# Weighing the expert activations on GpSimd and forming the low halves of the products on VectorE

## The chip, the cores and the metric

The kernel runs on one core of one Trainium2 chip. The metric is the device time of one execution in microseconds (us). The engines are TensorE (PE in the profile; PEld is its weight load), VectorE (DVE), ScalarE (ACT), GpSimd (POOL) and SyncE (SP, whose queue issues the DMAs). Each engine works through its own instructions in order, and semaphores order the engines among each other.

## What is computed

A gated linear attention layer and a mixture-of-experts feed-forward layer, each with a residual and a layer norm behind it. The input is 16 batches of 512 tokens of width 128. The change touches only the feed-forward part, in the reference:

```python
scores = jax.nn.softmax(xt @ gate_w.T, axis=-1)
topv, topi = jax.lax.top_k(scores, K)                 # K = 4 of E = 8 experts
topv = topv / jnp.sum(topv, axis=-1, keepdims=True)
combine = zeros((t, E)).at[arange(t)[:, None], topi].set(topv)
g = _silu(jnp.einsum('td,edh->eth', xt, exp_w1))
u = jnp.einsum('td,edh->eth', xt, exp_w3)
yexp = jnp.einsum('eth,ehd->etd', g * u, exp_w2)
routed = jnp.einsum('te,etd->td', combine, yexp)
shared = _silu(xt @ sh_w1) * (xt @ sh_w3) @ sh_w2     # two more experts' worth, not weighed
```

In front of it stand a linear and a gated layer (folded into one, "head"), behind it the same again ("tail"), then the second layer norm.

## The kernel before

The attention part runs first, for all 16 batches, and takes some 1,330 us. The expert stage follows, with one batch after the other. For each batch `n` it goes through ten slots `e` = 0 to 9: slots 0 and 1 are the two shared experts, slots 2 to 9 the eight routed ones. All tiles are 128 partitions by 512 tokens. In slot `e`:

- TensorE forms the two up projections, `up_gate` into `g_ps` and `up_linear` into `u_ps`, then the down projection `down` of the slot three back (`LAG` = 3). Each is three matmuls (L548 to L550), since every float32 operand is split into a high half and a low half: high by high, low by high, high by low.
- ScalarE takes silu of `g_ps` into `sg` (`silu_expert`, L1088), and then copies the product of the slot before, `gc`, into its high half `gc_part[0]` (`high_gc`, L1095).
- VectorE runs `gate_expert`: for a routed expert it multiplies `sg` by the combine weights `cw` (L1457, two inputs in SBUF), and then the result, or `sg` itself for a shared expert, by `u_ps` from PSUM (L1464), which gives `gc`.
- GpSimd subtracts the high half from `gc`, which gives the low half `gc_part[1]` (`low_gc`, L514, two inputs in SBUF).

Buffers tie the slots together: `sg`, `gu`, `g_ps` and `u_ps` are double, `gc` and its halves are fourfold. `up_linear` of slot `e` and silu of slot `e` wait for the product of slot `e` - 2; `down` of slot `e` - 3 waits for both halves. In the names of the trace `sq_sb` is `sg`, `kt_sb` and `s_sb` are `gu`, `v_sb` is `gc`, `wq` and `wk` (`_hi`, `_lo`) are `gc_part`, `ew_raw` and `e_sb` hold `cw`: the stage uses buffers of the attention part again.

Between the slots every engine does work for the neighbours. On VectorE, in this order, for the next batch: in slot 0 the low half of the head's input (L1374), in slot 2 the head's gated product (L1381, after `low_r`, L1393, of the batch before), in slot 3 its low half (L1388), in slot 4 the logits (L1401, L1404), in slots 5 to 7 the top-4 choice (L1417 to L1443, which ends with `comb`). For the batch before: in slot 3 the layer norm's output for two batches back (L1359, four instructions), in slot 6 the tail's gated product (L1593), in slots 8 and 9 the layer norm's sums and variance. ScalarE takes the exponential of the logits in slot 5 (L1082) and the tail's silu right behind it (L1110), each with a table load in front, and in slot 9 copies the transposed weights (L1100). SyncE stores these to DRAM and reads them back spread over all partitions into `cw` for slots 2 and up of the next batch (`spread_weights`, L389). GpSimd has one more instruction per batch, the `rstd` of the layer norm (L495), in slot 9.

## Time and profile before

| | us |
|---|---|
| median of 3 runs | 1809.33 (1806.43 to 1810.18) |
| the profiled execution | 1802.53 |
| its span, first to last instruction | 1800.8 |
| granted TensorE clock, mean | 0.994 of full speed |
| PE busy | 1673.4 (93%) |
| DVE busy | 1446.7 (80%) |
| ACT busy | 1107.5 (61%) |
| POOL busy | 614.3 (34%) |

The profile covers one execution. Busy shares are means over two very different stages, so they say little about the expert stage by themselves: there POOL is busy for about half of the time and DVE for more than eight tenths. The views that matter are those that can be asked for a stretch: the busy time per window, the waits, the chain that ended last in order of time, and the timeline of each engine. The durations of PE instructions are modelled and overlap; the start-to-start distance is the better measure of TensorE's pace.

### The profile page before, as it was taken

What the parts mean: (1) busy time and instruction counts of PE and PEld (TensorE: products, weight loads), DVE (VectorE), ACT (ScalarE), POOL (GpSimd) and SP (SyncE); (2) the same over time, 40 slices, a digit from 0 to 9 for tenths busy, and PEclk for the clock granted to TensorE, in tenths of its full rate; (3) what the DMA queues carried; (4) which work ended last, traced back from release to release, by engine and by line L of the source; (5) the groups of instructions that cost most, each with busy time, mean ns of one, the idle gap of its engine ahead of it and who ended that gap; (6) DMA issues with size and microseconds to landing.
All of it is one profiled execution on the core that took longest, in us unless ns stands there. A gap on an engine that the chain in (4) does not pass through costs nothing.

```text
span 1800.8 us, 83833 instructions
## 1 busy us (share of the span) xinstructions
PE 1673.4 (93%) x36615; PEld 1352.1 (75%) x36615; DVE 1446.7 (80%) x3326; ACT 1107.5 (61%) x2544; POOL 614.3 (34%) x470
## 2 busy tenths in 40 slices
PE   6999999999999999999999999999989999999996
PEld 5777777777777777777777778777777777777775
DVE  4888888787878878878878788877877888888886
ACT  5666566666666656666566666666655665666653
POOL 3323232232322233222322233222314554545544
PEclk9999999999999999999999999999999999999998
DMA  7000000000000000000000000000012322223222
GB/s 217 4 9 10 4 9 4 10 4 9 4 9 10 4 10 3 9 4 9 4 9 10 4 9 4 9 4 10 4 60 68 103 107 71 107 74 115 106 66 65
DMA packets 38139, 60.95 MB, mean 34 GB/s; under 512 B 3080, under 2 KB 24848, under 8 KB 37776
## 3 DMA queue, kind: packets, MB, share of 16 engines
q1 hardware_dynamic: 37776, 55.59, 9.3%
q8 instruction: 291, 4.77, 1.1%
q14 instruction: 72, 0.59, 0.1%
HBM read 46.93 MB, written 4.46 MB: 29 GB/s over the span
## 4 chain that ended last, share of the span: by engine, by line
PE 50%; DVE 24%; issue 11%; ACT 10%; DMA 3%; DVEq 0%; POOL 0%; ACTq 0%; SPq 0%; POOLq 0%
PE bank L641 7%; PE bank L548 7%; PE bank L676 6%; PE bank L550 6%; PE bank L549 6%; PE bank L690 5%; DVE k_sb L1283 5%; PE bank L587 4%; ACT v_sb L1017 3%; PE bank L663 3%; PE bank L624 3%; DVE kt_sb L1457 3%; DVE v_sb L1464 2%; DVE qq_sb L1283 2%; DMA ew_raw<-cw_dram 2%
## 5 line engine op out<-in xcount | busy, mean ns | idle before, releaser
L479 POOL TENSOR_TENSOR rn_sb<-ss_sb,expo 128x8 f32<-128x8 f32 x128 | 213.6, 1669 | 764.1 <-DVE ss_sb L1328 764.1
L1283 DVE TENSOR_TENSOR qq_sb<-qq_sb,tot_sb 128x512 f32<-128x512 f32 (+1 forms) x384 | 259.1, 675 | 231.7 <-PE bank L641 168.9
L1283 DVE TENSOR_TENSOR k_sb<-k_sb,tot_sb 128x512 f32<-128x512 f32 (+1 forms) x384 | 331.4, 863 | 1.3 <-PE bank L648 1.3
L1042 ACT ACTIVATE at_sb<-diag_sb 32x256 f32<-32x256 f32 x256 | 106.4, 416 | 164.8 <-DVE diag_sb L1295 160.1
L641 PEld LDWEIGHTS bank<-qq_sb,k_sb 128*32 128x32 f32 x12288 | 125.4, 110 | 62.9 <-issue 50.5
L514 POOL TENSOR_TENSOR wq_lo<-v_sb,wq_hi 128x512 fp32r<-128x512 f32 x80 | 112.2, 1406 | 132.7 <-ACT wq_hi L1095 132.7
L1017 ACT ACTIVATE v_sb<-bank,rn_sb 128x128 f32<-128x128 f32 x512 | 139.5, 384 | 26.6 <-PE bank L550 19.7
L323 POOL TENSOR_TENSOR tot_sb<-a_sb 128x512 f32<-128x512 f32 x64 | 96.1, 1502 | 167.0 <-ACT a_sb L1006 154.0
L641 PE MATMUL bank<-qq_sb,k_sb 128*32 128x16 f32 x12288 | 146.3, 185 | 6.9 <-issue 5.4
L548 PE MATMUL bank<-wg_hi,ew_hi 128*128 128x512 f32 x320 | 135.3, 423 | 15.8 <-DVE v_sb L1464 15.6
L690 PE MATMUL bank<-v_sb,at_sb 128*128 128x128 f32 x1024 | 148.1, 287 | 1.3 <-issue 1.0
L514 POOL TENSOR_TENSOR wk_lo<-v_sb,wk_hi 128x512 fp32r<-128x512 f32 x80 | 111.9, 1403 | 107.6 <-ACT wk_hi L1095 107.6
L587 PEld LDWEIGHTS bank<-ones_wide,sq_sb 128*32 128x32 f32 x8192 | 92.0, 111 | 62.0 <-issue 39.6
L1006 ACT ACTIVATE a_sb<-bank 128x512 f32<-128x512 f32 x128 | 76.6, 599 | 88.3 <-PE bank L550 79.6
L690 PEld LDWEIGHTS bank<-v_sb,at_sb 128*128 128x128 f32 x1024 | 124.2, 191 | 7.4 <-issue 1.7
L587 PE MATMUL bank<-ones_wide,sq_sb 128*32 128x1 f32 x8192 | 115.7, 173 | 11.6 <-issue 9.8
L549 PE MATMUL bank<-wg_lo,ew_hi 128*128 128x512 f32 x320 | 126.1, 394 | 0.0
L550 PE MATMUL bank<-wg_hi,ew_lo 128*128 128x512 f32 x320 | 126.1, 394 | 0.0
L1088 ACT ACTIVATE sq_sb<-bank 128x512 f32<-128x512 f32 x160 | 94.7, 592 | 49.5 <-PE bank L550 49.0
L676 PE MATMUL bank<-v_sb,kt_sb 128*128 128x128 f32 x768 | 119.9, 292 | 0.2
L700 PE MATMUL bank<-s_sb,qq_sb 128*128 128x128 f32 x768 | 113.3, 284 | 0.3
L988 ACT ACTIVATE k_sb<-bank 128x512 f32<-128x512 f32 x128 | 76.8, 600 | 55.3 <-PE bank L550 55.3
(195 smaller groups left out, 4254.3 us busy)
## 6 DMA issues: line engine op xcount, KB each, us to landing
ew_raw<-cw_dram SPq DMA_DIRECT2D x32, 768.0 KB, 6.2
x_nat<-in_L_attn_x_dram SPq DMA_DIRECT2D x16, 256.0 KB, 2.8
x_nat<-x_all SPq DMA_DIRECT2D x16, 256.0 KB, 2.5
ew_raw<-cw_dram SPq DMA_DIRECT2D x16, 256.0 KB, 3.9
e_sb<-cw_dram SPq DMA_DIRECT2D x16, 256.0 KB, 7.0
out_dram<-k_sb SPq DMA_DIRECT2D x16, 256.0 KB, 2.3
ew_raw<-in_L_ffn_exp_w_dram SPq DMA_DIRECT2D x3, 512.0 KB, 4.8
qq_sb<-in_L_attn_Wq_dram SPq DMA_DIRECT2D x1, 512.0 KB, 3.9
```

Source lines behind the costliest of these rows:

```text
L479: nc.gpsimd.tensor_tensor(rn_sb[par][:, i, :, :].rearrange("p h c -> p (h c)"), ss_sb[:, i * G:(i + 1) * G], expo[:, 0:G], ALU.pow).then_i ...
L514: nc.gpsimd.tensor_tensor(gc_part[1][(par * NE + e) % 4], gc[(par * NE + e) % 4], gc_part[0][(par * NE + e) % 4].bitcast(fp32), ALU.subtra ...
L548: nc.tensor.matmul(out_ap, stat(0), mov(0), start=start, stop=False)
L549: nc.tensor.matmul(out_ap, stat(0), mov(1), start=False, stop=False)
L550: return nc.tensor.matmul(out_ap, stat(1), mov(0), start=False, stop=stop)
L587: mm = nc.tensor.matmul((nb_ps, su_ps)[i][n * SB:(n + 1) * SB, col:col + 1], sq_sb[:, i * HP + h, lo:lo + SB], ones_wide[:, 0:1], start=Tr ...
L641: mm = nc.tensor.matmul(out[n * SB:(n + 1) * SB, g * HB:(g + 1) * HB], k_sb[par][:, left:left + SB], halves(qd_sb[par][:, left:left + SB], ...
L676: mm = nc.tensor.matmul((su_ps, kt_ps)[h][:, c * D:(c + 1) * D], kt_sb[:, h, c, :], v_sb[par][:, c, h * D:(h + 1) * D], start=True, stop=True)
L690: nc.tensor.matmul(y_ps[:, c * D:(c + 1) * D], at_sb[par][:, h * NC + c, :], v_sb[par][:, c, h * D:(h + 1) * D], start=p == 0 and h == 0 a ...
L700: mm = nc.tensor.matmul(y_ps[:, c * D:(c + 1) * D], qd_sb[par][:, lo:lo + C], s_sb[:, h, c - 1, :], start=False, stop=p == NP - 1 and h == ...
L1017: last = nc.scalar.activation(v_sb[par][:, c, h * D:(h + 1) * D], pj[n][:, at:at + D], ACT.Copy, scale=rn_sb[par][:, 1, h, c:c + 1])
L1283: return nc.vector.tensor_tensor(view, view, by, ALU.mult)
```

## The change

In the expert stage two elementwise instructions change places. The multiplication of `sg` by `cw` (eight per batch) goes from VectorE to GpSimd (`weigh`), and the subtraction that forms the low half of `gc` (ten per batch) goes from GpSimd to VectorE (`low_gc`). On VectorE the subtraction of slot `e` - 1 stands right behind the product of slot `e`, ahead of the slot's other work. The semaphore of the low halves (`p_gc`, now `v_lo`) is the same in all but its name. In the first batch `weigh` also waits in slots 2 and 3 until the attention part has read the buffers that `gu` shares with it.

```diff
-            def low_gc(n, par, e):
+            def weigh(n, e):
                 k = n * NE + e
-                pool.wait_ge(a_gc, k + 1)
-                nc.gpsimd.tensor_tensor(gc_part[1][(par * NE + e) % 4], gc[(par * NE + e) % 4], gc_part[0][(par * NE + e) % 4].bitcast(fp32), ALU.subtract).then_inc(p_gc, 1)
+                pool.wait_ge(a_sg, k + 1)
+                if e == NS:
+                    pool.wait_ge(cw_in[0], (n + 1) * 16)
+                elif e < NS + HE:
+                    pool.wait_ge(cw_in[1], (n + 1) * 16)
+                else:
+                    pool.wait_ge(cw_in[2], (n + 1) * 32)
+                pool.wait_ge(v_gu, k - 1)
+                if n == 0 and e < 4:
+                    pool.wait_ge(av_done, B * NP * HP)
+                nc.gpsimd.tensor_tensor(gu[e % 2], sg[e % 2], cw[e - NS], ALU.mult).then_inc(v_mid, 1)
...
                     for e in range(NE):
-                        low_gc(b + par, par, e)
+                        if e >= NS:
+                            weigh(b + par, e)
...
             def gate_expert(n, par, e):
                 k = n * NE + e
                 dve.wait_ge(a_sg, k + 1)
-                if e >= NS:
...
-                    nc.vector.tensor_tensor(gu[e % 2], sg[e % 2], cw[e - NS], ALU.mult).then_inc(v_mid, 1)
                 dve.wait_ge(f_u, k + 1)
-                await_count(dve, p_gc, k - 3)
+                await_count(dve, v_lo, k - 3)
                 if e >= NS:
                     dve.wait_ge(v_mid, n * E + e - NS + 1)
                 src = gu[e % 2] if e >= NS else sg[e % 2]
                 nc.vector.tensor_tensor(gc[(par * NE + e) % 4], src, u_ps[e % 2][:, :], ALU.mult).then_inc(v_gu, 1)
+
+            def low_gc(n, par, e):
+                k = n * NE + e
+                dve.wait_ge(a_gc, k + 1)
+                nc.vector.tensor_tensor(gc_part[1][(par * NE + e) % 4], gc[(par * NE + e) % 4],
+                                        gc_part[0][(par * NE + e) % 4].bitcast(fp32), ALU.subtract).then_inc(v_lo, 1)
...
                         if n > 0 or e >= 2:
                             gate_expert(n, par, e)
+                        if e > 0:
+                            low_gc(n, par, e - 1)
+                        elif has_prev:
+                            low_gc(n - 1, 1 - par, NE - 1)
                         if e == at_x and has_next:
                             head_x(n + 1)
...
             ffn(B - 2, last=True)
+            low_gc(B - 1, 1, NE - 1)
             ln2_out(B - 2, 0)
```

## Rows read from the trace of the kernel before

**Rows 1.** Busy time per window: window and length, then per engine busy us (instructions).

```profile
1600.00:1700.00 100.00, 95.70 (x440) 73.91 (x439) 86.00 (x179) 61.83 (x103) 52.69 (x39) 1.00 0.24 85
```

**Rows 2.** Waits of PE, 1350 to 1750 us: waiter, releaser, total us, times, longest.

```profile
PE bank L548 <- DVE v_sb L1464: 14.1, 38, 0.6
```

**Rows 3.** Chain that ended last, in order of time, 1350 to 1750 us: start, length, what.

```profile
1410.47 0.70 DVE kt_sb L1457
...
1573.07 1.99 DVE k_sb L1359 x4
1577.63 0.83 issue
...
1581.21 0.70 DVE kt_sb L1457
...
1609.09 0.70 DVE kt_sb L1457
...
1618.83 3.82 DMA ew_raw<-cw_dram
...
1749.78 0.70 DVE kt_sb L1457
```

**Rows 4.** Groups by line and shape, 1380 to 1760 us: count, busy us, mean ns, idle before.

```profile
L514 POOL TENSOR_TENSOR wq_lo<-v_sb,wq_hi 128x512 fp32r<-128x512 f32 x67 | 93.9, 1406 | 87.9 <-ACT wq_hi L1095 87.9
...
L1457 DVE TENSOR_TENSOR kt_sb<-sq_sb,ew_raw 128x512 f32<-128x512 f32 x54 | 48.7, 901 | 28.4 <-ACT sq_sb L1088 20.6 <-DMA ew_raw<-cw_dram 7.7
...
L1457 DVE TENSOR_TENSOR s_sb<-sq_sb,ew_raw 128x512 f32<-128x512 f32 x40 | 32.4, 810 | 0.0
...
L1457 DVE TENSOR_TENSOR s_sb<-sq_sb,e_sb 128x512 f32<-128x512 f32 x14 | 16.4, 1168 | 0.0
...
L1388 DVE TENSOR_TENSOR wg_lo<-k_sb,wg_hi 128x512 fp32r<-128x512 f32 x13 | 12.0, 923 | 0.0
```

**Rows 5.** Line L1464 over the whole span: ns minimum/median/maximum.

```profile
L1464 DVE TENSOR_TENSOR v_sb<-kt_sb,bank x64: 686/687/689, 1338.8 to 1779.4; 128x512 f32<-128x512 f32 x64
```

**Rows 6.** Timeline of DVE, 1566 to 1592 us and once 1768 us: start, length, instruction [idle before].

```profile
1566.92 1.76 DVE L1457 TENSOR_TENSOR kt_sb<-sq_sb,ew_raw 128x512 f32<-128x512 f32 x1 [0.49 <-ACT sq_sb L1088]
1568.81 0.69 DVE L1464 TENSOR_TENSOR v_sb<-kt_sb,bank 128x512 f32<-128x512 f32 x1
...
1570.67 0.68 DVE L1457 TENSOR_TENSOR s_sb<-sq_sb,ew_raw 128x512 f32<-128x512 f32 x1
1571.49 0.69 DVE L1464 TENSOR_TENSOR v_sb<-s_sb,bank 128x512 f32<-128x512 f32 x1
1572.09 0.97 DVE L1388 TENSOR_TENSOR wg_lo<-k_sb,wg_hi 128x512 fp32r<-128x512 f32 x1
...
1576.61 0.19 DVE L1404 TENSOR_TENSOR lg<-bank,lmax 128x32 f32<-128x32 f32 x1
...
1581.21 0.69 DVE L1457 TENSOR_TENSOR kt_sb<-sq_sb,ew_raw 128x512 f32<-128x512 f32 x1 [1.27 <-ACT sq_sb L1088]
1582.04 0.69 DVE L1464 TENSOR_TENSOR v_sb<-kt_sb,bank 128x512 f32<-128x512 f32 x1
...
1591.05 0.69 DVE L1464 TENSOR_TENSOR v_sb<-s_sb,bank 128x512 f32<-128x512 f32 x1
...
1767.89 1.27 DVE L1359 TENSOR_SCALAR k_sb<-res,mean,rstd 128x128 f32<-128x128 f32 x4
```

**Rows 7.** Timeline of POOL, the same stretch.

```profile
1566.81 3.01 POOL L514 TENSOR_TENSOR wq_lo<-v_sb,wq_hi 128x512 fp32r<-128x512 f32 x2
...
1589.07 1.30 POOL L514 TENSOR_TENSOR wq_lo<-v_sb,wq_hi 128x512 fp32r<-128x512 f32 x1 [0.42 <-ACT wq_hi L1095]
```

**Rows 8.** Timeline of ACT, the same stretch.

```profile
1569.75 0.60 ACT L1088 ACTIVATE sq_sb<-bank 128x512 f32<-128x512 f32 x1
...
1577.17 1.28 ACT L1082 ACT_TABLE_LOAD   x1
...
1580.59 0.59 ACT L1088 ACTIVATE sq_sb<-bank 128x512 f32<-128x512 f32 x1
```

More of the change, by code:

```diff
@@ L277, in gated_linear_attention_and_moe_block @@
         a_gc = sem("a_gc")
-        p_gc = sem("p_gc")
+        v_lo = sem("v_lo")
         f_ct = sem("f_ct")
@@ L768, in down @@
             def down(n, par, e):
-                pe.wait_ge(p_gc, n * NE + e + 1)
+                pe.wait_ge(v_lo, n * NE + e + 1)
                 if e == 0:
@@ L1449, in gate_expert @@
                 dve.wait_ge(a_sg, k + 1)
-                if e >= NS:
-                    if e == NS:
-                        dve.wait_ge(cw_in[0], (n + 1) * 16)
-                    elif e < NS + HE:
-                        dve.wait_ge(cw_in[1], (n + 1) * 16)
-                    else:
-                        dve.wait_ge(cw_in[2], (n + 1) * 32)
-                    nc.vector.tensor_tensor(gu[e % 2], sg[e % 2], cw[e - NS], ALU.mult).then_inc(v_mid, 1)
                 dve.wait_ge(f_u, k + 1)
-                await_count(dve, p_gc, k - 3)
+                await_count(dve, v_lo, k - 3)
                 if e >= NS:
```

## The prediction

> **What bounds the kernel now.** I read the busy time per window first. In a full window of the expert stage TensorE is busy for 95.7 of 100 us and VectorE for 86.0, ScalarE for 61.8, GpSimd for 52.7 [rows 1]. So two engines are close to full and the busy shares don't tell which one sets the end. The waits of TensorE come next: for the first matmul of a group it waits 38 times for VectorE's product, 14.1 us in all over 400 us [rows 2]. That is small, but it says that TensorE is at times ahead of VectorE and not the other way. The chain in order of time decides: over the stage it runs along VectorE, then ScalarE, then VectorE again, and through the DMA of the combine weights; TensorE is hardly on it. The same piece, the weighing of slot 6 at L1457, comes back in each batch: at 1581.21 and 1609.09, so one lap is 27.88 us. From 1410.47 to 1749.78 there are 12 laps, 28.3 us each, since a few are held up by the DMA [rows 3].
>
> How a lap goes is best seen with a clock of its own, zero at the end of slot 6's silu, 1581.19 (L1088, 1580.59 and 0.59) [rows 8]. VectorE has been idle for 1.27 us before it. It weighs slot 6 and forms its product at 0.85 (1582.04), and goes on without a gap to the product of slot 9, which ends at 10.55 (1591.05 and 0.69) [rows 6]. The chosen weights go out to DRAM and back and bring the next weighing, slot 2, at about 14: the chain has a DMA piece there from 1618.83 on, 3.82 long, which ends 13.6 after the start of its lap at 1609.09 [rows 3]. For the rest of the lap I take the rows of the batch that ended in this silu, moved by one lap. The product of slot 2 starts at 15.5 (1568.81), the weighing of slot 3 at 17.4, its product at 18.2, the logits are out at 23.5 (1576.61 and 0.19) [rows 6]. ScalarE starts the table load for the exponential at 23.9 (1577.17) [rows 8]; load, exponential, load, tail silu and slot 6's silu follow back to back and end at 27.9. This is the loop that I reckon with.
>
> **Part one: the weighing goes to GpSimd.** VectorE loses 8 instructions per batch of 0.69 us when undisturbed, and the wait between weighing and product: start to start they are 0.83 apart (1581.21, 1582.04) [rows 6], where independent instructions follow in 0.60 (1571.49 to 1572.09) [rows 6]. So each weighing occupies 0.83 us. It also loses what they suffer from GpSimd: their means are 901, 810 and 1168 ns over 54, 40 and 14 of them [rows 4], 903 ns together, 0.21 over the undisturbed 0.69, so 1.7 us per batch. The worst one shows how: it starts at 1566.92 and takes 1.76, while GpSimd is at work from 1566.81 [rows 6, 7]; an instruction of VectorE with two inputs in SBUF stands still until GpSimd's instruction is through. The product, which reads one input from PSUM, never does: 686 to 689 ns in 64 cases [rows 5].
>
> The Trainium skill states this as a rule (SBUF — State Buffer, Who interferes with whom): VectorE with two SBUF inputs and GpSimd reading SBUF exclude each other for a whole instruction, and issue order decides who waits. The rows above agree. It speaks against the change, since the subtraction too has two SBUF inputs: the ones exposed on VectorE go from eight to ten, with eight instead of ten on GpSimd to meet. By the rule alone the sum stays open, as it names no order.
>
> In place of it the weighing takes GpSimd 1.30 us undisturbed (1589.07) and 1.41 on average, if the multiplication costs what the subtraction does [rows 7, 4]. The trace has no multiplication of this shape there; same shape, same inputs, so I take 1.30 and for the range 1.3 to 1.8 (1.3 plus part of a VectorE instruction in front). With a hand-over of 0.1 on either side (an estimate: VectorE to itself takes 0.83 - 0.69 = 0.14 [rows 6]) silu to product is 1.5 where it was 0.85. This lies on the path wherever VectorE is waiting for silu, and beside other work elsewhere. GpSimd's only other instruction, the `rstd` in slot 9, may now be queued behind a weighing, 1.3 us; its reader comes in slot 3 of the next batch, so nothing.
>
> **Part two: the subtraction goes to VectorE.** Ten per batch. The nearest row is L1388, the same shape, inputs and output: 923 ns on average over 13 [rows 4], of which 0.97 at 1572.09 [rows 6] is a blocked one. Undisturbed I take 0.60 start to start. TensorE gets it sooner in principle (0.69 for 1.30), but `down` runs three slots late, so that is worth nothing. Queued behind it are the slot's own tasks: logits, choice, tail product. VectorE's sum per batch without collisions is 8 x 0.83 = 6.6 off and 10 x 0.60 = 6.0 on: 0.6 us less. This must not be read as a gain: two subtractions fall in slots 0 and 1, where nothing was removed.
>
> **The lap again, by hand.** From zero: GpSimd weighs slot 6 from 0.1 to 1.4, the product starts at 1.5 (+0.6). Slot 5's subtraction wants 2.1 but meets slot 7's weighing, 1.4 to 2.7, and ends at 3.2. The choice's second step and the tail product follow, the latter at 4.6 instead of 3.3. Slots 7 to 9 get back what was lost, for their weighings are gone; one more subtraction is blocked, in slot 8, for 0.6. Product 9 ends at 10.5: no change. So the weights leave for DRAM at the same time within 0.1, and are back at 13.6 to 14. GpSimd weighs slot 2 until 15.3 (VectorE took as long, blocked by GpSimd, [rows 6]); slot 0's subtraction, late by then, meets it. Product 2 starts at 15.8 to 16.2, +0.3 to +0.7. Two subtractions more ahead of slot 3, and its weighing: silu of slot 3 ends at 17.1 in the rows (1569.75 and 0.60, moved by a lap [rows 8]), some 0.2 later with TensorE's lag; so weighing until 18.7 and product 3 at 18.8, +0.6. Then to the end of the logits the rows take 5.3 us (18.2 to 23.5). After: products 3 and 4, subtractions 2 and 3 and L1388 at 0.6 make 3.0; L1359's four take 1.99 on the chain [rows 3] but 1.27 when GpSimd is quiet [rows 6], so 1.2; logits 0.4; 4.6 in all. Into this stretch fall GpSimd's weighings of slots 4 and 5, 2.6 us, and everything in it but the products and the logits can be blocked. I take one of the two as met, 1.3; the bounds are none (0) and nearly both (2.2). So the logits are out at 18.8 + 4.6 + 1.3 = 24.7. ScalarE waited until 23.9 for product 4 anyway, so the load is 0.8 late, and the zero of the next lap with it. With product 2 at the upper value and slot 6's subtraction once more blocked it is 1.7; with nothing met it is 0 (then 23.4, hidden behind ScalarE).
>
> I take **+0.9 us per lap**. Fifteen laps (batches 1 to 15) make +13.5. At the end the last subtraction is 0.69 us instead of 1.30, and slot 9's weighing is later by 0.1: -0.5. Ahead of the first lap slots 0 and 1 of batch 0 have slack in TensorE's three-slot delay; 0 to +1. Sum **+14 us** against the profiled 1802.5, which makes 1816.5. The median of the runs, 1809.3, is 6.8 above the profiled execution; the forecast for the median is **1823 us**.
>
> **The rivals.** *Faster.* VectorE is the engine of the chain and gets 0.6 us less work per batch plus the 1.7 us of collisions. If GpSimd's weighings fall under the products and under waits of VectorE, the subtractions stay clean and product 3 is not held, the stretch from product 2 to the logits (7.0 us clean after 15.8) ends at 22.8 instead of 23.5, and product 4 is earlier too: about -0.7 per lap, -10 in all: 1799. It decides at the point whether slot 3's weighing is done before VectorE has finished the head's product (about 18.2). For it speak 14.1 us of TensorE's waits for VectorE that could be won [rows 2]; against it that silu 3 ends at 17.1 at best, and 17.1 + 1.5 is 18.6.
>
> *No change.* The lap closes through the DMA (slot 6 to slot 9, out and back), and what is lost behind it hides in ScalarE's 0.4 us of waiting and in collisions that only change sides. 1809, within 3.6.
>
> *Much slower.* The blocked instruction is the rule: VectorE now sends its subtraction right behind the product, when ScalarE has released the next weighing. Each of ten subtractions meets half of a weighing, 0.65, and L1359 all of one: some 2.5 per lap, +38: 1847. It decides when the two engines fall into step. Against it: in slots 0 and 1 GpSimd has nothing to do.
>
> **How the numbers follow.** The forecast case (0.2 to 1.7 per lap, 1812 to 1835) gets 0.52, much slower 0.10, no change 0.15, faster 0.23. Anything within 0.2% (3.6 us) is about what a measurement of this kernel can't tell from no change. Slower is 0.52 + 0.10 = 0.62. The range leaves out the outer halves of the outer cases: from 1801 (0.11 below) to 1838 (0.08 above).
>
> **What would show it.** In the profile after: the idle time of VectorE ahead of the product (L1464) with GpSimd's weighing as the releaser, in slots 3 and 6; a mean of the subtraction on VectorE well over 0.69, near 0.9; the distance from slot 6's silu to its product at 1.5; a lap near 28.8 where it was 27.88; TensorE's waits in the stage up from 14 us. It would be wrong if GpSimd's multiplication took a different time than its subtraction, if laps became shorter, if the subtraction's mean stayed at 0.7, or if VectorE's collisions in the logits' stretch were gone.

## The result, and the profile after the change

The changed kernel takes 1811.72 us (median of 20 runs, 1808.87 to 1816.15), the kernel before 1806.56 us in 20 runs beside it (1801.57 to 1811.10). The ratio is 1.0031, with a 95% interval from 1.0022 to 1.0039: slower by 5.2 us, where 14 were forecast. The profiled execution of the changed kernel has a span of 1809.9 us; that of the kernel before had 1800.8. The difference of these two, 9.1, is larger than the one of the medians, and a part of it lies where nothing was changed (below).

From the page of the kernel after the change, the busy time of each engine:

```profile
PE 1675.8 (93%) x36615; PEld 1354.9 (75%) x36615; DVE 1455.2 (80%) x3358; ACT 1108.6 (61%) x2544; POOL 566.8 (31%) x438
```

The busy times per window, kernel after (window, its length, then PE, PEld, DVE, ACT and POOL, the granted clock, the DMA share, GB/s). The first is the window of [rows 1]; the other two are the places at either end of the stage to which the experiments led:

```profile
1600.00:1700.00 100.00, 95.00 (x436) 74.38 (x436) 87.64 (x180) 64.42 (x106) 41.87 (x33) 1.00 0.29 102
1350.00:1354.00 4.00, 4.00 (x12) 3.13 (x11) 1.49 (x3) 1.12 (x2) 0.00 (x0) 0.58 0.01 5
1772.00:1776.00 4.00, 2.57 (x6) 2.12 (x7) 3.51 (x8) 0.11 (x1) 0.14 (x1) 0.65 0.11 37
```

In the middle little has moved: TensorE 95.0 for 95.7, VectorE 87.6 for 86.0, GpSimd 41.9 for 52.7. In the two short windows TensorE's granted clock is 0.58 and 0.65, so it ran mostly at 1.2 GHz and not at 2.4.

The waits, kernel after, 1350 to 1750 us (waiter, releaser, total us, times, longest), which answer to [rows 2]:

```profile
DVE v_sb L1466 <- POOL kt_sb L523: 31.0, 17, 2.1
DVE v_sb L1466 <- POOL s_sb L523: 12.5, 18, 1.3
...
PE bank L558 <- DVE wvo_lo L1403: 5.9, 13, 1.2
PE bank L558 <- DVE v_sb L1466: 5.3, 12, 0.9
...
PE bank L558 <- issue: 3.7, 1, 3.7
```

VectorE's product (L1466) now waits 43.5 us for GpSimd's weighing (L523). TensorE waits less often for the product, 12 times in place of 38, but it has a wait that was smaller before: 3.7 us in one piece, put down to "issue" (2.0 in the kernel before, shown with e7). All its waits of this view together are 24.0 us; in the kernel before they were 20.6.

The groups by line and shape, kernel after, 1400 to 1750 us (count, busy us, mean ns), which answer to [rows 4, 5]:

```profile
L523 POOL TENSOR_TENSOR kt_sb<-sq_sb,ew_raw 128x512 f32<-128x512 f32 x50 | 69.9, 1397 | 83.0 <-ACT sq_sb L1098 79.2 <-DMA ew_raw<-cw_dram 3.8
L1472 DVE TENSOR_TENSOR wq_lo<-v_sb,wq_hi 128x512 fp32r<-128x512 f32 x63 | 59.1, 939 | 0.0
L1472 DVE TENSOR_TENSOR wk_lo<-v_sb,wk_hi 128x512 fp32r<-128x512 f32 x63 | 57.7, 916 | 0.0
...
L1466 DVE TENSOR_TENSOR v_sb<-kt_sb,bank 128x512 f32<-128x512 f32 x50 | 34.0, 681 | 24.4 <-POOL kt_sb L523 24.0 <-PE bank L560 0.3
...
L1398 DVE TENSOR_TENSOR wg_lo<-k_sb,wg_hi 128x512 fp32r<-128x512 f32 x13 | 8.9, 684 | 0.0
```

The subtraction that moved (L1472) takes 0.93 us on VectorE on average, the weighing on GpSimd 1.36 over all its 99 in this stretch (1.29 to 1.40 by buffer). The product stays at 681 ns. The head's subtraction (L1398, L1388 before) fell from 923 to 684 ns: its collisions are gone.

Now one lap. Timeline of VectorE, kernel after (start, length, instruction, idle time before it and its releaser), the place of [rows 6]:

```profile
1560.62 0.69 DVE L1466 TENSOR_TENSOR v_sb<-kt_sb,bank 128x512 f32<-128x512 f32 x1 [1.90 <-POOL kt_sb L523]
1561.23 1.05 DVE L1472 TENSOR_TENSOR wk_lo<-v_sb,wk_hi 128x512 fp32r<-128x512 f32 x1
...
1562.98 0.74 DVE L1602 SCALAR_TENSOR_TENSOR qq_sb<-bank,swf_b,qq_sb 128x512 f32<-128x512 f32 x1
...
1569.10 0.67 DVE L1466 TENSOR_TENSOR v_sb<-s_sb,bank 128x512 f32<-128x512 f32 x1
...
1574.79 0.67 DVE L1466 TENSOR_TENSOR v_sb<-kt_sb,bank 128x512 f32<-128x512 f32 x1
...
1577.87 0.69 DVE L1466 TENSOR_TENSOR v_sb<-s_sb,bank 128x512 f32<-128x512 f32 x1 [0.55 <-POOL s_sb L523]
...
1579.08 0.68 DVE L1398 TENSOR_TENSOR wg_lo<-k_sb,wg_hi 128x512 fp32r<-128x512 f32 x1
1579.68 2.07 DVE L1369 TENSOR_SCALAR k_sb<-res,mean,rstd 128x128 f32<-128x128 f32 x4
1581.67 0.67 DVE L1466 TENSOR_TENSOR v_sb<-kt_sb,bank 128x512 f32<-128x512 f32 x1
1582.27 1.67 DVE L1472 TENSOR_TENSOR wk_lo<-v_sb,wk_hi 128x512 fp32r<-128x512 f32 x1
...
1584.06 0.19 DVE L1414 TENSOR_TENSOR lg<-bank,lmax 128x32 f32<-128x32 f32 x1
...
1588.54 0.69 DVE L1466 TENSOR_TENSOR v_sb<-kt_sb,bank 128x512 f32<-128x512 f32 x1 [1.88 <-POOL kt_sb L523]
```

From the product of slot 6 to the next one: 1588.54 - 1560.62 = 27.92 us. A lap was 27.88 [rows 3]. The prediction wanted 28.8.

ScalarE's timeline in the same lap, kernel after, which answers to [rows 8]:

```profile
1582.37 0.63 ACT L1105 ACTIVATE wq_hi<-v_sb 128x512 fp32r<-128x512 f32 x1 [0.36 <-DVE v_sb L1466]
1583.03 1.28 ACT L1092 ACT_TABLE_LOAD   x1
1584.32 0.23 ACT L1092 ACTIVATE ex<-lg 128x32 f32<-128x32 f32 x1
```

GpSimd's timeline in the same lap, kernel after, which answers to [rows 7]:

```profile
1559.19 1.29 POOL L523 TENSOR_TENSOR kt_sb<-sq_sb,ew_raw 128x512 f32<-128x512 f32 x1 [3.75 <-ACT sq_sb L1098]
...
1579.13 1.76 POOL L523 TENSOR_TENSOR kt_sb<-sq_sb,ew_raw 128x512 f32<-128x512 f32 x1 [1.40 <-ACT sq_sb L1098]
```

The table load starts at 1583.03, while the logits end only at 1584.25 (1584.06 and 0.19). It did not wait for them. It follows at once on ScalarE's copy of product 4 (L1105, 1582.37), which had waited for that product (1581.67 and 0.67).

### Where the time went

The exponential of the choice runs once per batch, 16 times, and cuts the expert stage at the same place in each kernel. I read its start from ScalarE's timeline in every profile; this table is worked out from those starts (us). "Laps" are the distances from one exponential to the next, 15 in all.

| profile | first exponential at | first lap | laps 2 to 15, sum | the usual lap | last exponential to the end |
|---|---|---|---|---|---|
| before | 1325.6 | 25.99 | 395.4 | 27.88 | 53.8 |
| before, again (e1) | 1332.5 | 24.23 | 393.5 | 27.87 | 52.6 |
| after | 1333.0 | 28.17 | 391.1 | 27.93 | 57.6 |
| after, again (e11) | 1332.7 | 27.96 | 390.9 | 27.93 | 57.4 |

With two profiles of each program: the first lap has become 3.0 us longer (28.07 for 25.11), the end 4.3 us (57.5 for 53.2), and laps 2 to 15 together 3.5 us shorter (391.0 for 394.5). That makes +3.8 us from the first exponential on (means of the whole stretch: 476.6 for 472.7), beside +5.2 in the medians. The start of the stage at 1325.6 or 1332.5 is the same program twice, so the 7.4 us between the starts of the first two profiles compared say nothing of the change. With two profiles of each, a difference of one or two us in one of these marks is not settled: the first lap of the same program is 25.99 and 24.23. TensorE's clock goes with it: in the first of the two it is granted 0.57 from 1341 to 1345 us, behind a wait of 2.00, and in the second, behind one of 1.78, it is at 1.00 (1347 to 1351).

That the laps are shorter in sum, though the usual one is 0.05 longer, is due to a few late ones in the kernel before: 28.2 (third lap), 29.6 (seventh) and 29.2 (fifteenth) in each of its profiles, and 29.6 (eighth) in one. The changed kernel has none but a 28.2 in lap 13.

### The profile page after: what moved, and what is told of

Its sections match the earlier page's. It is cut to its first block, busy times and chain, and to the rows that moved or that the text cites. A ratio compares the mean times of both kernels' runs of the same rounds, so it can differ in the third digit from the quotient of the medians.

```text
span 1809.9 us, 83961 instructions
## 1 busy us (share of the span) xinstructions
PE 1675.8 (93%) x36615; PEld 1354.9 (75%) x36615; DVE 1455.2 (80%) x3358; ACT 1108.6 (61%) x2544; POOL 566.8 (31%) x438
## 4 chain that ended last, share of the span: by engine, by line
PE 53%; DVE 21%; issue 14%; ACT 8%; POOL 2%; DMA 2%; DVEq 0%; POOLq 0%; SPq 0%; ACTq 0%
PE bank L558 8%; PE bank L651 7%; PE bank L560 7%; PE bank L559 6%; PE bank L686 6%; DVE k_sb L1293 5%; PE bank L700 5%; PE bank L597 4%; ACT v_sb L1027 3%; PE bank L673 3%; PE bank L634 3%; DVE qq_sb L1293 2%; DVE v_sb L1466 2%; PE bank L710 2%; ACT at_sb L1052 2%
## 5 line engine op out<-in xcount | busy, mean ns | idle before, releaser
L1098 ACT ACTIVATE sq_sb<-bank 128x512 f32<-128x512 f32 x160 | 94.9, 593 | 53.6 <-PE bank L560 52.7
L523 POOL TENSOR_TENSOR kt_sb<-sq_sb,ew_raw 128x512 f32<-128x512 f32 x64 | 89.0, 1390 | 117.5 <-ACT sq_sb L1098 111.7
L686 PEld LDWEIGHTS bank<-v_sb,kt_sb 128*128 128x128 f32 x768 | 95.7, 191 | 3.3
```

The costliest lines, as they stand in the source:

```text
L686: mm = nc.tensor.matmul((su_ps, kt_ps)[h][:, c * D:(c + 1) * D], kt_sb[:, h, c, :], v_sb[par][:, c, h * D:(h + 1) * D], start=True, stop=True)
```

## The experiments

All comparisons are ratios to the kernel before, run on the same chip, with 95% intervals. No kernel here leaves out any of the computation. Line numbers in rows are those of each kernel itself.

### The two kernels once more: how much is chance (e1, e11)

e1 is the kernel before with no edit, e11 the changed kernel with no edit.

> The kernel before, unchanged, profiled a second time. Two theories of where the change's 0.31% comes from. Theory A (the ends): the laps of the expert stage are as long as before (27.93 us with the change, 27.87 without, but for a few held up by the DMA), and the loss is in the first and the last batch, where TensorE stands still and its clock falls. The attention part, whose code the change doesn't touch, then differs between the two profiles (exponential of the first logits' table load at 1324.3 us before, 1331.8 after) only because executions differ: A expects this second look at 1324 to 1332 for the same mark, with all the expert stage's laps at 27.9 but for some late DMAs. Theory B (the unchanged part): the attention part is slower in the changed program, by its layout or otherwise: B expects 1323 to 1326 here again.

Measured: 1804.49 us, the kernel before beside it 1803.66; span 1802.8. The first exponential is at 1332.5, where the first profile had 1325.6. So what spoke for the theory that the unchanged attention part costs the change some us (B) falls away: the same program has that scatter. A part of the 1.4 us by which the medians differ more than the stage does (5.2 and 3.8) is not excluded by it. Its late laps stand in the same places.

> The change once more, unaltered, beside the others on one chip. Theory A: laps of 27.9 us, first lap and end again longer than in the kernel before by 2 to 5 us each (28 to 29.5, and 57 to 58), none of the laps over 28.5 but the first two; ratio 1.002 to 1.004. If the ends of the first profile were chance: first lap under 27 or end under 56.

Measured: 1811.74 us, ratio 1.0037 (1.0023 to 1.0051), span 1808.9. First lap 27.96, end 57.4, usual lap 27.93: the three marks of the change repeat within 0.25 us.

### Do one part of the change alone (e2, e3)

In e2 VectorE does both, the weighing and the subtraction; GpSimd keeps only `rstd`:

```diff
@@ gate_expert, ahead of the product
+                if e >= NS:
+                    ... the three waits on cw_in, as in weigh
+                    nc.vector.tensor_tensor(gu[e % 2], sg[e % 2], cw[e - NS], ALU.mult).then_inc(v_mid, 1)
@@ ffn, on GpSimd
-                        if e >= NS:
-                            weigh(b + par, e)
```

> One part alone: VectorE forms the low halves as in the change, and also keeps the weighing as in the kernel before; GpSimd has only the layer norm's power left. So there are next to no collisions in the expert stage. By the prediction's prices VectorE gets 10 x 0.60 = 6.0 us more per batch and loses 1.7 us of collisions; it was idle for about 3 us of a lap of 27.9, not all of it usable. Theory A: a lap of 29 to 30 us, 1.0 to 1.5% slower than before. Rival (collisions are the price of the change, not the amount of work): no slower than the change, 1.003 or less. Laps tell: over 28.8 for A, under 28.3 for the rival.

Measured: 1815.93 us, ratio 1.0071 (1.0053 to 1.0090), span 1812.6; the usual lap is 28.79. Groups by line and shape of e2, 1400 to 1750 us:

```profile
L1478 DVE TENSOR_TENSOR wq_lo<-v_sb,wq_hi 128x512 fp32r<-128x512 f32 x62 | 42.5, 685 | 0.0
```

The subtraction takes 685 ns in place of 939: without GpSimd there is no collision left. Yet each lap is 0.86 longer than in the changed kernel. So a lap without collisions can be longer than one with them: the work on VectorE costs more here. Ten subtractions of 0.60 (start to start) were 6.0 us more than before, and 0.9 of it came out as time; where it comes out is read below, with e5.

In e3 GpSimd does both, and VectorE only the product:

```diff
@@ on GpSimd, behind each weighing
+                        if e > 0:
+                            low_gc(b + par, par, e - 1)
+                        elif not (first and par == 0):
+                            low_gc(b + par - 1, 1 - par, NE - 1)
@@ on VectorE
-                        if e > 0:
-                            low_gc(n, par, e - 1)
-                        elif has_prev:
-                            low_gc(n - 1, 1 - par, NE - 1)
```

> The other part alone: GpSimd weighs as in the change, and also keeps the low halves as in the kernel before (weighing of slot e, then the low half of slot e - 1). VectorE gets 8 x 0.83 = 6.6 us less per batch and nothing instead; GpSimd has 18 x 1.30 + 1.0 = 24.4 us of a lap of 27.9. If the latency of silu to product (1.5 for 0.85) costs more than VectorE's lighter load gives: a lap of 28.0 to 28.6, 1.003 to 1.015. If VectorE's load sets the lap: 27.0 to 27.5, ratio 0.985 to 0.995. I lean to the first, 1.005, for GpSimd's subtractions stand behind weighings and TensorE's down projection then waits for them.

Measured: 1833.71 us, ratio 1.0175 (1.0152 to 1.0199), span 1831.4; laps of 29.7 to 30.3. That was far above what I expected. The waits of e3, 1400 to 1750 us, say why:

```profile
DVE v_sb L1476 <- POOL kt_sb L523: 70.5, 24, 3.5
...
DVE v_sb L1476 <- POOL s_sb L523: 16.6, 33, 1.3
```

VectorE waits 87 us for GpSimd, up to 3.5 at a time. Eighteen instructions of 1.3 us in a batch are 23 us of a 28 us lap, and a weighing now queues behind a subtraction that nobody is in a hurry for. I had added up GpSimd's load and not asked what stands in front of each weighing. Moving the weighing alone (1.0175) is thus the worse half, moving the subtraction alone costs as well (1.0071), and the two together cost less than either (1.0031 and 1.0037).

### What the late logits cost (e5)

The prediction worked out the logits' end in a lap at 24.7 after silu 6, and the trace has 25.1. But the lap hardly grew (27.93 for 27.88). Two waits stand ahead of the exponential in ScalarE's program, for the logits and for the choice's weights of the batch before. e5 swaps them; nothing else changes:

```diff
-                act.wait_ge(v_lg, n + 1)
...
+                act.wait_ge(v_lg, n + 1)
```

> The change with ScalarE's two waits ahead of the exponential issued in the other order, so that the table load in front of it waits for the logits, and not only for the combine weights of the batch before, as it does now. In the prediction the load was held by the logits, and 0.8 us of the forecast 0.9 per lap came from there. In the profile of the change the load starts at 23.9 after slot 6's silu, as before, while the logits end at 25.2. If that is the step that failed, this kernel must show the loss that was forecast: laps of 29.0 to 29.4 us (the load 1.2 us later, 27.93 + 1.2 = 29.1), 1.011 to 1.015 against before. Rival: the lap is set elsewhere (TensorE's pace, the DMA of the weights) and the load has slack: laps stay under 28.2, ratio 1.003 to 1.005.

Measured: 1824.40 us, the kernel before 1803.80, ratio 1.0104 (1.0079 to 1.0128); span 1825.7, laps of 29.2. ScalarE's timeline of e5, two laps:

```profile
1562.78 1.28 ACT L1092 ACT_TABLE_LOAD   x1 [1.31 <-DVE lg L1414]
...
1592.02 1.28 ACT L1092 ACT_TABLE_LOAD   x1 [1.36 <-DVE lg L1414]
```

Here the load waits 1.3 us for the logits and the lap is 1.27 longer. In the changed kernel the load does not wait for the logits and runs beside them, 1.28 us, and the exponential follows at 1584.32, 0.07 behind the logits. The kernel before has the waits in the same order; its logits were early in each of the sixteen batches, so one could not see it there. This is the step of the prediction that failed, measured by itself.

What the lap does follow can be read from the timelines of VectorE and ScalarE in every profile. This table is worked out from them: medians over the laps from the second on, in us after the end of silu 6.

| profile | product 4 starts | table load starts | logits end | lap |
|---|---|---|---|---|
| before | 22.49 | 23.87 | 23.50 | 27.88 |
| after | 22.57 | 23.93 | 25.14 | 27.94 |
| e8 | 22.42 | 23.77 | 25.00 | 27.78 |
| e2 | 23.41 | 24.78 | 25.02 | 28.79 |
| e4 | 23.78 | 25.14 | 25.38 | 29.15 |
| e3 | 24.34 | 25.70 | 25.34 | 29.71 |
| e5 | 22.56 | 25.21 | 25.13 | 29.22 |

In all but e5 the load follows product 4 by 1.35 to 1.38 us and the lap is 5.4 longer than the time to product 4, wherever the logits end. The subtractions count for the lap as far as they stand ahead of product 4 and push it back: by 0.1 in the changed kernel, by 0.9 in e2. In the changed kernel the blocked subtraction at 1582.27 stands behind product 4, so it delays the logits alone.

### The last batch (e6)

In the last batch TensorE waits for `wvo_lo`, the low half that L1403 forms. TensorE's timeline, kernel after:

```profile
1773.43 0.77 PE L558 MATMUL bank<-wk_hi,ew_hi 128*128 128x512 f32 x1 [2.59 <-DVE wvo_lo L1403]
```

VectorE's timeline there, kernel after:

```profile
1770.76 0.69 DVE L1466 TENSOR_TENSOR v_sb<-kt_sb,bank 128x512 f32<-128x512 f32 x1 [1.29 <-POOL kt_sb L523]
1771.37 1.32 DVE L1472 TENSOR_TENSOR wk_lo<-v_sb,wk_hi 128x512 fp32r<-128x512 f32 x1
1772.61 0.68 DVE L1403 TENSOR_TENSOR wvo_lo<-bank,wvo_hi 128x512 fp32r<-128x512 f32 x1
```

L1403 stands behind a product that waits for GpSimd's weighing, and behind the subtraction of slot 1, which the weighing of slot 3 blocks: 1.32 in place of 0.69. e6 moves L1403 ahead of that subtraction, in the last batch alone:

```diff
+                        if e == 2 and last and par == 1:
+                            low_r(n - 1)
                         ... low_gc ...
-                        if e == 2 and has_prev:
+                        if e == 2 and has_prev and has_next:
```

> The change with low_r ahead of slot 1's subtraction in the last batch only. With it in all batches the laps grew from 27.9 to 29.1 us, since slot 4's weighing then starts ahead of the head's low half (L1398) and blocks it; the part from the last exponential to the end fell from 57.6 to 53.2 us. So A (the ends) expects here laps of 27.9 as in the change and an end of 53 to 55 us: 1.000 to 1.0015 against before. If the shorter end there was luck (an undisturbed clock) or is bound to the longer laps, the end stays at 56 to 58 and the ratio at 1.003.

Measured: 1805.56 us, ratio 1.0006 (0.9993 to 1.0020), span 1805.8. The end, from the last exponential on, is 54.8 where the changed kernel had 57.6 and 57.4. TensorE's timeline of e6:

```profile
1770.89 0.47 PE L558 MATMUL bank<-wk_hi,ew_hi 128*128 128x512 f32 x1 [1.39 <-DVE wvo_lo L1403]
```

The busy times of the window around it, e6:

```profile
1770.00:1774.00 4.00, 3.11 (x14) 2.62 (x15) 4.00 (x9) 1.75 (x3) 1.59 (x2) 1.00 0.25 87
```

The wait is 1.39 and the clock behind it 1.00, where it was 2.59 and 0.65. In the kernel before this wait was 1.29, TensorE's timeline:

```profile
1766.70 0.47 PE L548 MATMUL bank<-wk_hi,ew_hi 128*128 128x512 f32 x1 [1.29 <-DVE wvo_lo L1393]
```

So 1.2 us of the 2.7 gained are the wait itself; the rest is what the clock would explain, which was low in the changed kernel's window and lengthened the matmuls (0.77 for 0.47 in the first). The end in e6 is still 1.6 longer than the 53.2 of the kernel before. A second stretch at the low clock is left there, which e6 has as the changed kernel has it (0.51 from 1789 to 1796 us). The window, kernel after:

```profile
1793.00:1800.00 7.00, 5.09 (x12) 2.79 (x10) 2.68 (x9) 0.60 (x1) 1.39 (x1) 0.55 0.13 37
```

In e1 twelve matmuls at this place (1786 to 1793) are busy for 3.55 us at a clock of 1.00. Why the clock falls there is not settled: e4 has the same waits ahead of it (1.73 and 0.40) and keeps 1.00. Not all of the gain at the end is seen in the whole stage: e6's first two laps, which have no edit, are 29.3 and 28.5, 2.0 us longer than in the changed kernel's first profile. Batch 0 scatters.

### Both ends (e7)

In batch 0 there is a like place. TensorE's timeline, kernel before:

```profile
1340.23 0.47 PE L548 MATMUL bank<-xT_hi,swf_hi 128*128 128x512 f32 x1 [2.00 <-issue]
```

TensorE's timeline, kernel after, the same matmul:

```profile
1349.65 0.49 PE L558 MATMUL bank<-xT_hi,swf_hi 128*128 128x512 f32 x1 [3.73 <-issue]
```

VectorE's timeline ahead of it, kernel after:

```profile
1347.13 0.69 DVE L1466 TENSOR_TENSOR v_sb<-kt_sb,bank 128x512 f32<-128x512 f32 x1 [2.23 <-POOL kt_sb L523]
1347.74 1.21 DVE L1472 TENSOR_TENSOR wq_lo<-v_sb,wq_hi 128x512 fp32r<-128x512 f32 x1
1348.87 0.68 DVE L1384 TENSOR_TENSOR xT_lo<-bank,xT_hi 128x512 fp32r<-128x512 f32 x1
```

GpSimd's timeline at that time, kernel after:

```profile
1344.38 1.39 POOL L495 TENSOR_TENSOR rstd<-ve,expo 128x4 f32<-128x4 f32 x1 [30.82 <-DVE ve L1364]
1345.74 1.26 POOL L523 TENSOR_TENSOR kt_sb<-sq_sb,ew_raw 128x512 f32<-128x512 f32 x1
```

TensorE stands 3.73 us for the head's low half (L1384). That one is queued on VectorE behind product 2, product 2 waits for GpSimd's weighing of slot 2, and that is queued behind `rstd` on GpSimd. Behind product 2 comes a blocked subtraction, 1.21. Counted from the first exponential, the low half starts at 15.8 where it was 13.85; product 2 starts 0.85 later than in the kernel before, and the subtraction adds 1.1. Behind the wait the clock is 0.58 for 4 us, as it was 0.57 in the first profile of the kernel before. e7 has e6's edit and two in batch 0: the head's low half ahead of product 2, and `rstd` behind the weighing of slot 3:

```diff
-                        if e == 1 and first and par == 0:
+                        if e == 3 and first and par == 0:
                             ln_rstd(B - 1)
...
+                        if e == at_x and n == 0:
+                            head_x(n + 1)
                         ... gate_expert, low_gc ...
-                        if e == at_x and has_next:
+                        if e == at_x and has_next and n > 0:
                             head_x(n + 1)
```

> As e6, and in batch 0 the low half of the head's input (L1384) ahead of product 2, and the layer norm's power on GpSimd behind the weighing of slot 3 in place of slot 1. In the change's batch 0 TensorE stands for 3.7 us for that low half, which waits behind product 2, GpSimd's weighing and a blocked subtraction; the clock is at 0.58 for 4 us after it. A expects the part from the first exponential to the second to fall from 28.2 to 25 to 26.5 us, the end as in e6, and laps as in the change: 0.997 to 1.0005 against before, no slower. If the cost is spread over the laps or lies in the attention part: 1.002 or more.

Measured: 1800.48 us, the kernel before 1803.80, ratio 0.9980 (0.9965 to 0.9996), span 1799.1. The first lap is 24.2 (28.2 and 28.0 in the changed kernel), the end 54.8, the usual lap 27.93 as before. VectorE's timeline of e7:

```profile
1341.00 0.68 DVE L1384 TENSOR_TENSOR xT_lo<-bank,xT_hi 128x512 fp32r<-128x512 f32 x1
```

The busy times per window, e7:

```profile
1342.00:1346.00 4.00, 3.47 (x16) 2.51 (x15) 2.98 (x4) 1.71 (x4) 3.38 (x3) 1.00 0.98 352
```

The low half is formed ahead of the product's wait, and the clock stays at 1.00. The move of `rstd` has little part in it: without `rstd` in front, the weighing of slot 2 waits for the DMA of its weights and starts 12.4 after the first exponential, where it was 12.7. Three edits that touch two of sixteen batches take out more than the whole loss: from 1.0031 or 1.0037 to 0.9980.

### Is it the change that brings this, or the edit? (e10)

The same edit of batch 0 in the kernel before:

```diff
@@ kernel before
+                        if e == at_x and n == 0:
+                            head_x(n + 1)
                         ...
-                        if e == at_x and has_next:
+                        if e == at_x and has_next and n > 0:
```

> A control: the kernel before, with the low half of the head's input ahead of the weighing and the product of slot 2 in batch 0, as in the re-ordered ends. It tells whether that gain belongs to the change (whose weighing goes the longer way round over GpSimd) or was open to the kernel before as well. If it belongs to the change: the first lap stays at 24 to 26 us, 0.9985 to 1.0005. If it was open anyway: first lap under 23.5 us, 0.996 to 0.998. In either case the laps of 29.6 and 29.2 us should be back in the 7th and the 15th place, if they belong to the program of before and not to chance.

Measured: 1800.93 us, the kernel before 1804.29, ratio 0.9981 (0.9970 to 0.9993), span 1796.0; first lap 22.84 in place of 26.0 and 24.2. So e7 beats the kernel before, but not by the change: the kernel before with one edit of its own is as fast. Of the 3.9 us that e7 gains in the first lap, the same edit gives the kernel before 2.3 (25.1 to 22.8). With batch 0 mended in both, and the last batch in e7 as well, the change is worth nothing that these runs can tell. The edit of the last batch was not tried in the kernel before, where the wait is only 1.29. The late laps (28.2, 29.6, 29.2) are all there in e10.

### Order in the other batches (e4, e8, e9)

e4 moves L1403 ahead of the subtraction in slot 2 in every batch, as TensorE waits for it in every lap (5.9 us over 13 laps, shown above):

```diff
+                        if e == 2 and has_prev:
+                            low_r(n - 1)
                         ... low_gc ...
-                        if e == 2 and has_prev:
-                            low_r(n - 1)
```

> The change with the low half of the tail's input (low_r) put ahead of the subtraction of slot 1 in slot 2, in every batch. In the change's last batch TensorE waits 2.59 us for low_r, which stands behind a subtraction blocked by GpSimd (1.32 us), and its clock is at 0.65 in the 4 us that follow. Theory A: the wait in the last batch shrinks to about 1.3 us, no clock dip there, the last batch is 2 to 3.5 us shorter; laps the same; ratio to before 1.001 to 1.002. Theory B (the unchanged part), or a cost spread over the laps: ratio stays at 1.003.

Measured: 1826.09 us, ratio 1.0134 (1.0111 to 1.0158), span 1823.6; laps of 29.1 to 30.0. Both theories missed this, by a full microsecond per lap. VectorE's timeline of e4, in the stretch before the logits:

```profile
1587.27 1.76 DVE L1398 TENSOR_TENSOR wg_lo<-k_sb,wg_hi 128x512 fp32r<-128x512 f32 x1
1588.96 2.08 DVE L1369 TENSOR_SCALAR k_sb<-res,mean,rstd 128x128 f32<-128x128 f32 x4
```

ScalarE's timeline of e4, the copy of product 4 ahead of the table load:

```profile
1591.67 0.63 ACT L1105 ACTIVATE wq_hi<-v_sb 128x512 fp32r<-128x512 f32 x1 [2.12 <-DVE v_sb L1466]
```

GpSimd's timeline of e4, the same stretch:

```profile
1586.66 1.82 POOL L523 TENSOR_TENSOR kt_sb<-sq_sb,ew_raw 128x512 f32<-128x512 f32 x1 [0.73 <-ACT sq_sb L1098]
1589.62 1.33 POOL L523 TENSOR_TENSOR s_sb<-sq_sb,ew_raw 128x512 f32<-128x512 f32 x1 [1.14 <-ACT sq_sb L1098]
```

In the changed kernel GpSimd's weighing of slot 4 starts at 1579.13, at the same time as the head's subtraction L1398 (1579.08). L1398 goes through in 0.68, and GpSimd is the one that waits (1.76 for 1.29). In e4 the weighing starts at 1586.66, 0.61 ahead of L1398 (1587.27); now L1398 is blocked (1.76), and L1369 behind it by the next weighing (2.08). Both stand ahead of product 4 in VectorE's queue, so product 4 starts at 23.8 of the lap where it was 22.6, and ScalarE's copy of it waits for 2.12 us. The logits end only 0.2 later than in the changed kernel. Four laps of e4 (29.5 to 29.7) have a stretch at half the clock as well. The Trainium skill (SBUF — State Buffer, Who interferes with whom) says that issue order decides which of the two waits, and these two rows agree; what it makes of the time was not to be had from the rule. An instruction of 0.68 us was moved by one place and the lap lost 1.2 us.

e8 moves the subtraction of slot 5 ahead of product 6, into the time in which VectorE waits for GpSimd:

```diff
+                        if e == 6:
+                            low_gc(n, par, e - 1)
                         ... gate_expert ...
-                        if e > 0:
+                        if e == 6:
+                            pass
+                        elif e > 0:
```

> The change with the subtraction of slot 5 ahead of product 6, where VectorE is idle for 1.9 us in each lap while GpSimd weighs slot 6. ScalarE makes the high half of slot 5 only behind slot 6's silu, so the subtraction can't start before 0.6 after it, and by then GpSimd has the port until 1.4. If GpSimd's next weighing (slot 7) waits in turn, the subtraction is through at 2.0, product 6 at 2.6, and slot 6 ends 0.5 earlier than in the change: laps 27.4 to 27.9, ratio 0.997 to 1.003. If the second weighing goes first, product 6 is at 3.3 and TensorE's next slots wait for it: laps of 28.5 to 29.5, ratio 1.008 to 1.018. I lean to the first.

Measured: 1809.69 us, ratio 1.0020 (1.0005 to 1.0035), span 1808.6; the usual lap is 27.78. That is 0.15 less per lap, 2 us over laps 2 to 15. But the first two laps are 29.5 and 28.6 here, where the changed kernel has 28.2 and 27.6, so the stage as a whole is not shorter (477.4 us from the first exponential on, for 476.9 and 476.3), and the intervals of the two ratios overlap. The idle time of 1.9 us ahead of product 6 is therefore hardly on the path: filling it with a subtraction that otherwise takes 1.05 us behind the product gave 0.15.

e9 has the edits of e7 and e8 together.

> Both found gains together: the re-ordered ends (ratio 0.998, first lap 24.2, end 54.8 us) and the subtraction of slot 5 ahead of product 6 (laps of 27.78 us for 27.93). If they add up: laps of 27.8, the ends as before, 15 x 0.15 = 2.2 us less than with the ends alone: 0.9965 to 0.9975. If the laps fall into another order of collisions: 28.5 or more and a ratio over 1.003.

Measured: 1800.34 us, the kernel before 1804.29, ratio 0.9977 (0.9962 to 0.9991), span 1796.3. The laps are 27.78, as in e8, and the first is 24.0, but the end is 56.0 and the second lap 28.25 where e7 has 54.8 and 27.54. Nothing measurable is added to e7.

## Why the prediction was right or wrong

The sign came out, and 1811.7 lies within the range; the size did not: +14 us were forecast and +5.2 measured. The time is also just below the bounds of the forecast case (1812 to 1835), and the lap is: +0.05 where 0.2 to 1.7 were given. That the sum came out as near as it did is luck: nearly all of the forecast was in the laps, which lost nothing, and nearly all of the loss was at the ends, which were put at nothing. So it is made of two errors that partly cancelled.

- **GpSimd's multiplication at 1.30 us.** Right: 1.29 undisturbed at 1559.19, 1.36 on average.
- **Silu 6 to product 6, 1.5 us instead of 0.85.** Right. Silu 6 ends at 1559.1, GpSimd starts at 1559.19 and the product at 1560.62.
- **The subtraction on VectorE near 0.9, not 0.69.** Right: 939 and 916 ns. The subtraction next to product 6 is blocked and ends at 3.2 of the lap, as worked out.
- **The tail product at 4.6.** It is at 3.9: the choice's small instructions follow more closely than I had them. No consequence.
- **Product 9 at 10.5, product 2 at 15.8 to 16.2, product 3 at 18.8.** The trace has product 9 end at 10.65 (1569.10 and 0.67), product 2 at 15.7 (1574.79) and product 3 at 18.8 (1577.87 - 1559.1). Right within 0.15. The chain of the kernel after has no DMA of the combine weights in this lap.
- **The logits at 24.7.** They are out at 25.1. The row of the subtraction at 1582.27, 1.67 long, shows the one blocked instruction of this stretch, and the norm (L1369) at 2.07 another; two were met, not one.
- **"So the load is 0.8 late, and the zero of the next lap with it."** This is the step that failed. I took it that the table load waits for the logits, since it stands with the exponential. It starts at 1583.03, 23.9 of the lap, at the same point as before [rows 8], 1.2 us ahead of the end of the logits. What it waits for is ScalarE's copy of product 4, and product 4 stands ahead of the blocked subtraction: it starts at 22.55 where it was 22.48. The load of 1.28 covered what was late of the logits, to 0.07 us. e5, in which the load does wait, shows what the step would have been worth: +1.27 per lap and 1.0104, which lies in the forecast case (0.2 to 1.7 per lap). Had I asked which instruction of the pair carries which wait, the traces of before had no row to answer it (the logits were early by 0.4 us then: 1576.80 against 1577.17). It should have been a rival with its own price.
- **+0.9 per lap, 15 laps, +13.5.** The working gives 0.8; the other 0.1 has no term. Measured: 14 laps by +0.05 is +0.7. Against that stands a gain that no step had: the late laps of the kernel before are gone, so laps 2 to 15 are 3.5 us shorter in sum.
- **The ends, -0.5 and 0 to +1.** These are the mis-sized terms. The last stretch is 4.3 us longer and the first lap 3.0, so 7.3 in place of about 0. The prediction counted the last subtraction and slot 9's weighing at the end, and at the start put everything down to slack in TensorE's delay of three slots. That holds for `down`; it doesn't hold for the low halves of the head (L1384) and of the residual (L1403), which TensorE needs at once and which stand behind a product that now waits for GpSimd. e6 and e7 show it: with these two taken out from behind it, 2.7 and 3.9 us come back, a good part of it through the clock behind the waits.
- **The rule of the Trainium skill (SBUF — State Buffer, Who interferes with whom), exposed ones from eight to ten.** The trace agrees with the rule. But e2, which has no collision at all, is slower than the changed kernel, so the collisions were not what the comparison turned on.
- **The rival "faster", point of decision: is slot 3's weighing done before the head's product.** It is not. VectorE waits for it by 0.55 at 1577.87, as the point against it said.
- **The rival "no change"** had the mechanism for the laps in part: what is lost "hides in ScalarE's 0.4 us of waiting and in collisions that only change sides". What hid it was the load and not the waiting of 0.4, but for 14 of the 15 laps this rival is what happened. I gave it 0.15.
- **The rival "much slower"**, the two engines in step, did not come up in the changed kernel. e4 shows that it is one move of one instruction away, with 1.2 of the 2.5 us per lap that I had given it. The 2.5 itself was a guess: ten times 0.65 and L1359 are more, and no step says how much of it stands on the path.
- **The sign "TensorE's waits in the stage up from 14 us".** The 14.1 were its waits for the product, and these fell to 5.3. All its waits together rose, from 20.6 to 24.0, through those for `wvo_lo` and the one of 3.7.

What stays open. From the issue of the combine weights' store to the issue of the load that waits for it, SyncE's queue has 1.46 us in most batches. In the seventh batch it has 3.11, 2.92 and 2.85 in the three profiles of the kernel before and its edit e10, and in the eighth 2.57, 2.74 and 2.45; in those batches the profiles after, e11, e7 and e9 have 1.46 to 1.49, and only in the thirteenth 2.0 to 2.2 (the very first of the stage is late in all, 2.4 to 2.8). e3, in which GpSimd does the subtractions as before, has both late ones too (2.72 and 2.54). The lateness in the eighth batch lengthened the lap in one profile out of three only. Why the store is late there, and not in the changed kernel, is not settled, nor is the third lap of 28.2. The 29.2 us of lap 15 has a visible cause, a small instruction of the choice that met GpSimd, timeline of VectorE, kernel before:

```profile
1726.30 1.27 DVE L1443 TENSOR_TENSOR comb<-picked,rden 128x32 f32<-128x32 f32 x1 [0.25 <-DVE rden L1440]
```

In the lap shown of the kernel after it takes 0.19 (1565.48). Open too is why the attention part ends at anything from 1325.6 to 1333.0 us in the profiles of these kernels, in which it is not edited.

## What to carry to other kernels

When work is moved between engines, look first at what a late value meets on the way to the next lap; a late logit cost nothing here since the instruction that it delays has a table load in front of it that does not wait for it, and the lap followed product 4. Work out the first and the last batch by themselves with what their queues hold: 7.3 us were lost in the first lap and behind the last exponential, and nothing in the fourteen laps between. And before you say that a change gives a gain, put the neighbouring edit into the kernel before as well; here the edit of batch 0 gave the same ratio there (0.9981 and 0.9980).

## What the runs showed of the hardware

- A table load that precedes an activation did not take all of the two waits issued ahead of it. With the logits' wait written first the load ran ahead of the logits, by up to 1.3 us, and with it written last the load waited for them, and laps of 27.93 became 29.2. That it takes the wait written last in the first order too is not shown, since that one had long ended.
- An instruction on four tiles of 128x128 with one tensor input and one value per row for each of mean and rstd (L1369) is blocked by GpSimd as the ones with two large inputs are: 2.07 and 2.08 us with GpSimd at work, 1.27 when it is quiet [rows 6], 1.11 in e2, where GpSimd has next to nothing to do.
- TensorE's clock was at 0.65 over 4 us around a wait of 2.59 us, at 0.58 behind one of 3.73 and at 0.57 behind one of 2.00, and at 1.00 around one of 1.39 and behind one of 1.78. The first matmul behind the wait of 2.59 took 0.77 where it took 0.47 at the full clock. Making the wait 1.2 us shorter made the end 2.6 to 2.8 shorter (e6).
- GpSimd at 23 us of work in a lap of 28 was too full to be waited for: VectorE lost 87 us over 350.
